# Low part of the first output-weight block of each group on VectorE instead of GpSimd, in a fused attention and feed-forward kernel

## The reference

```
q, k, v = xn @ wq, xn @ wk, xn @ wv      # 32 query heads, 8 key/value heads, 128 wide
q, k = rope(q), rope(k)
s = softmax(q k^T / sqrt(128), causal and at most 127 tokens back) v     # per head
s = s @ wo                                # 4096 x 512
g = silu(ffn(xn))                         # ffn: W1, W3, W2 from packed 4-bit values and scales, hidden 1376
out = x + s * g
```

## Time and profile before

| | |
|---|---|
| median of 3 runs | 816.35 us (816.35, 816.83, 815.01) |
| the profiled execution's own time | 816.31 us |
| its span, first to last instruction | 814.5 us |
| mean granted TensorE clock | 0.998 of full speed |
| TensorE busy | 799.0 us (98%), 3928 matmuls |
| VectorE busy | 564.8 us (69%) |
| GpSimd busy | 484.3 us (59%) |
| ScalarE busy | 428.2 us (53%) |
| GpSimd L398 on output weights, groups 1 to 7 | 28 of them |
| GpSimd L398 on input weights, all | 40 of 1393 ns |
| DMA | 54.00 MB, mean 66 GB/s |

### The profile page before, as it was taken

One profiled execution on the slowest core, in us unless ns is written; L12 is line 12 of the kernel. 1 busy time (PEld: TensorE's weight loads), 2 busy tenths in 40 slices (PEclk: granted clock), 3 DMA queues, 4 the chain that ended last, 5 costly groups with the idle time before them and its releaser, 6 DMA issues.

```text
span 814.5 us, 13389 instructions
## 1 busy us (share of the span) xinstructions
PE 799.0 (98%) x3928; PEld 668.5 (82%) x3928; DVE 564.8 (69%) x1628; ACT 428.2 (53%) x1103; POOL 484.3 (59%) x362
## 2 busy tenths in 40 slices
PE   6999999999999999999999999999999999999987
PEld 4888888888888888888888888888888888888876
DVE  6625858576558867767686777768677676867774
ACT  4412313223138675666656576665656666665562
POOL 2112324224156774877488497747839774789985
PEclk9999999999999999999999999999999999999999
DMA  9449525211000400400030040003004001220102
GB/s 286 147 164 271 157 78 139 82 39 52 0 28 14 130 14 0 131 1 14 12 118 13 0 129 0 13 28 101 13 0 129 0 13 38 91 64 0 39 1 104
DMA packets 51908, 54.00 MB, mean 66 GB/s; under 512 B 4128, under 2 KB 33184, under 8 KB 51872
## 3 DMA queue, kind: packets, MB, share of 16 engines
q1 hardware_dynamic: 51584, 53.49, 22.0%
q10 hardware_dynamic: 288, 0.07, 0.0%
HBM read 47.25 MB, written 6.29 MB: 66 GB/s over the span
## 4 chain that ended last, share of the span: by engine, by line
PE 75%; POOL 15%; issue 6%; DVE 1%; ACT 1%; DMA 0%; POOLq 0%; ACTq 0%; DVEq 0%
PE bank L1270 20%; PE bank L1271 20%; PE bank L1272 20%; POOL wol L398 5%; POOL swap L424 5%; PE bank L1384 2%; PE bank L1397 2%; PE bank L1311 2%; PE bank L1316 2%; PE bank L1322 2%; POOL q L428 2%; POOL pl L447 1%; POOL ph L447 1%; POOL acc L455 1%; PE bank L1414 1%
## 5 line engine op out<-in xcount | busy, mean ns | idle before, releaser
L424 POOL TENSOR_TENSOR swap<-swap,cst 128x512 f32<-128x512 f32 x80 | 108.4, 1355 | 39.6 <-ACT swap L665 39.6
L686 ACT ACTIVATE probs<-probs,nmx 128x128 f32<-128x128 f32 x256 | 100.0, 392 | 60.4 <-DVE nmx L1055 60.4
L1270 PE MATMUL bank<-xh,wih 128*128 128x512 f32 x320 | 128.9, 403 | 0.0
L1271 PE MATMUL bank<-xl,wih 128*128 128x512 f32 x320 | 125.2, 391 | 0.0
L1272 PE MATMUL bank<-xh,wil 128*128 128x512 f32 x320 | 125.0, 391 | 0.0
L1270 PE MATMUL bank<-woh,oh 128*128 128x512 f32 x256 | 100.5, 392 | 0.1
L1271 PE MATMUL bank<-wol,oh 128*128 128x512 f32 x256 | 100.2, 391 | 0.0
L1272 PE MATMUL bank<-woh,ol 128*128 128x512 f32 x256 | 99.9, 390 | 0.0
L374 POOL TENSOR_TENSOR hl<-act_h,hh 128x512 fp32r<-128x512 f32 x22 | 32.0, 1454 | 102.2 <-ACT hh L564 102.2
L428 POOL TENSOR_TENSOR q<-q,swap 128x512 f32<-128x512 f32 x64 | 85.5, 1335 | 6.7 <-DVE q L1030 1.8
L447 POOL TENSOR_TENSOR ph<-ph,cst 128x512 fp32r<-128x512 f32 x32 | 42.8, 1338 | 72.0 <-ACT ph L701 72.0
(11 more groups left out here) (121 smaller groups left out, 2006.5 us busy)
## 6 DMA issues: line engine op xcount, KB each, us to landing
raw<-in_wq SPq DMA_DIRECT2D x32, 256.0 KB, 5.0
raw<-in_wo SPq DMA_DIRECT2D x32, 256.0 KB, 4.9
pk<-in_w SPq DMA_DIRECT2D x44, 128.0 KB, 3.7
sc<-in_s SPq DMA_DIRECT2D x44, 128.0 KB, 3.9
vals<-stage SPq DMA_DIRECT2D x16, 256.0 KB, 2.5
vraw<-vals SPq DMA_DIRECT2D x16, 256.0 KB, 3.0
pk<-in_w SPq DMA_DIRECT2D x11, 256.0 KB, 2.7
sc<-in_s SPq DMA_DIRECT2D x11, 256.0 KB, 3.0
```

Source lines behind the costliest of these rows:

```text
L424: nc.gpsimd.tensor_tensor(v, v, spread(sin.unsqueeze(1), P, 2, SEQ), ALU.mult).then_inc(sin_done, 1)
L686: e = nc.scalar.activation(probs[:, s, c0:c1], probs[:, s, c0:c1], ACT.Exp, bias=nmx[:, s, i:i + 1], scale=-1.0, accum_out=rsum[:, s, i:i ...
L1270: nc.tensor.matmul(out_, sh, mh, start=(i == 0), stop=False)
L1271: nc.tensor.matmul(out_, sh, ml, start=False, stop=False)
```

## The change

In groups 1 to 7 the low part of the first output-weight block (`wol[:, 0]`) is made by VectorE, behind its two `p_lo` and ahead of `cos_part`, in step `bp` = 0. GpSimd's loop over the four blocks begins at the second. In group 0 GpSimd still makes all four. The low part of slot 5 counts a semaphore of its own, `wl_here`, on either engine, so that `wl_done` counts eight per group, and all waits on it are renumbered. SP and TensorE wait for `wl_here` where they need that block.

```diff
@@ constants
-ALL_W = CHUNKS * NKV
+LOWS = CHUNKS - 1
@@ semaphores
-        wh_done, wl_done = sem("wh_done"), sem("wl_done")
+        wh_done, wl_done, wl_here = sem("wh_done"), sem("wl_done"), sem("wl_here")
@@ counts
+        def wo_low(g, h):
+            return LOWS * g + (5 + h - 1)
+        def in_low(g, c):
+            return LOWS * g + c
@@ SP, group_loads
-                        wait(sp, wl_done, wo_chunk(g, h) - RING + 1)
+                        if h == 0:
+                            sp.wait_ge(wl_here, g)
+                        else:
+                            wait(sp, wl_done, wo_low(g - 1, h) + 1)
                         load_wo(5 + h, g, h)
...
-                        wait(sp, wl_done, in_chunk(g + 1, c) - RING + 1)
+                        wait(sp, wl_done, in_low(g, c) + 1)
                         load_in(c, g + 1, c)
@@ SP, reload of x at the end
-                sp.wait_ge(wl_done, ALL_W + t - RING + 1)
+                if t == 5:
+                    sp.wait_ge(wl_here, NKV)
+                else:
+                    sp.wait_ge(wl_done, (in_low(NKV - 1, t) if t < 5 else wo_low(NKV - 1, t - 5)) + 1)
@@ GpSimd, w_lo
-                nc.gpsimd.tensor_tensor(lo, raw[:, slot, :], hi.bitcast(f32), ALU.subtract).then_inc(wl_done, 1)
+                nc.gpsimd.tensor_tensor(lo, raw[:, slot, :], hi.bitcast(f32), ALU.subtract) \
+                    .then_inc(wl_here if slot == 5 else wl_done, 1)
@@ GpSimd, step
                 if w:
-                    for h in range(GH):
+                    for h in range(1, GH):
                         lo_wo(g, h)
@@ VectorE
+            def first_wo_lo(g):
+                dve.wait_ge(wh_done, wo_chunk(g, 0) + 1)
+                nc.vector.tensor_tensor(wol[:, 0, :], raw[:, 5, :], woh[:, 0, :].bitcast(f32),
+                                        ALU.subtract).then_inc(wl_here, 1)
@@ VectorE, step
                 p_lo(g, bp, 0, 0)
                 p_lo(g, bp, 0, 1)
+                if bp == 0:
+                    first_wo_lo(g)
                 cos_part(ng, nbp, 0)
@@ TensorE, project
-                    pe.wait_ge(wl_done, in_chunk(g, c) + 1)
+                    pe.wait_ge(wl_done, in_low(g, c) + 1)
@@ TensorE, out_project
                 if bp == 0 and t == 0:
-                    pe.wait_ge(wl_done, wo_chunk(g, GH - 1) + 1)
+                    pe.wait_ge(wl_here, g + 1)
+                    pe.wait_ge(wl_done, wo_low(g, GH - 1) + 1)
```

## The result

The changed kernel took 812.16 us (median of 6 runs, 811.16 to 813.01), the kernel before 816.82 in the runs beside it: ratio 0.9945, 95% interval 0.9930 to 0.9959. That is 4.7 us by the medians. The profiled execution took 811.49 us with a span of 809.7.

A forecast was written before the change was run, and what follows sets the result against it. TensorE, busy in 98% of the span, was taken as the bound, waiting for GpSimd's late masked copy. Six turns 2.7 + last group 1.0 + clock 1.4 = 5.1 us; 816.3 - 5.1 = 811.2 us, range 809.9 to 814.0.

The forecast's parts named there:

- The six turns: Groups 1 to 6: TensorE's 0.50 us wait per turn for GpSimd's masked copy shrinks by 0.45; 2.7 us (1.8 to 3.0).
- the last group: Group 7: GpSimd loses one of four low parts, so L1423 comes 0.9 to 1.4 us earlier; taken as 1.0 us.
- The clock term: TensorE's clock fall behind the last group's waits may not come: 1.4 us or nothing; clock still falling had chance 0.27.
- The next candidate: Product at 422.85, needing VectorE's low part from 421.50 to 422.19; moved up by 0.50, its start and that part are level.
- Only 0.6 of the 1.4 us come through: First masked copy, now at 419.15, can't start before 418.55 because of ScalarE's high part; GpSimd waits for the rest.
- VectorE for nothing in groups 1 to 6: Moved subtraction fits VectorE's 2.65 us gap behind the first two turned blocks; 0.68 to 1.34 us long, costed at nothing.
- The point from which it is paid: Slower outcome decides if the moved subtraction takes over 2.5 us or ScalarE's high part comes over 1.7 us after 398.8.
- The slower rival: VectorE becomes late, delaying key rotation, masking and low parts; 3.9 us over seven groups, 820.2 us; chance 0.05.
- Contention, up to 0.46, swallowed by the idle time: Moved instruction slows GpSimd's masked copy at 399.66 by up to 0.46 us; 0.82 us idle behind it absorbs that.
- the likeliest case: The forecast itself, 811.2 us, with the six turns, the last group and the whole clock term; chance 0.50.

The follow-up runs named there:

- half a block in place of a whole one: Kernel before, nothing moved; from group 1 on GpSimd makes only 256 of 512 columns of the first output-weight block's low part; 811.95 us (one run).
- the run with one column: Changed kernel with VectorE making only one of the 512 columns of the moved low part; 811.13 us, ratio 0.9944.
- last group undone: Changed kernel, but in group 7 GpSimd makes all four low parts, as before; 813.59 us, ratio 0.9969.
- the last two kernels: Changed kernel with two rest products behind the last group's last rotation, 809.84 us; then all four there and some sums moved later too, 809.20 us.

## Why the prediction was right

The forecast was 811.2, the profiled execution took 811.49 and the median is 812.16, in the stated range. The six turns and the last group came out as worked out. The clock term did not, and that the total is so close is in part luck.

- *Six turns, 2.7 us (1.8 to 3.0).* Measured 2.8 to 2.9, near the upper end: 0.49 per turn and not 0.45. The next candidate, VectorE's low part at 421.50, now ends at 420.83 + 0.69 = 421.52, and the product that needs it starts at 421.67 with no wait shown. It was level, as said, and TensorE did not have to wait for it.
- *Only 0.6 of the 1.4 us come through.* Right in kind: GpSimd waits 0.67 us in front of the masked copy, and half a block in place of a whole one gives 70.29. What comes off GpSimd behind the low parts is 1.7 us and not 1.3 to 1.5. The wait for ScalarE's swap, 0.58 us, was not in the working; it changed nothing, since the copy of the high part comes later still.
- *VectorE for nothing in groups 1 to 6.* Shown by the run with one column (0.53 us less, no gain) and by the run that does it twice (1.66 us more, no cost). The duration was 1.17 in the loop, 1.60 in the last group, of the 0.7 to 1.8 allowed. The point from which it is paid was put at 2.5 us of length; two instructions of 2.9 us together are still free in the loop, three of 4.6 cost 1.85 per turn.
- *The slower rival.* It did not come about, but its mechanism is real: 0.46 us over the kernel before when the instruction stands one place later, where the price worked out was 0.55 per group.
- *Contention, up to 0.46, swallowed by the idle time.* 0.44 in the loop, swallowed. In the last group it was paid: the copy takes 1.75 us and not 1.28, and the one-column run, which spares that, has L1445 0.37 us earlier.
- *The last group, 1.0 us.* 0.93.
- *The clock, 1.4 us or nothing.* This term was mis-sized. TensorE's clock did not fall in the profiled execution (granted 1.00 from 775 to 778 us), and L1445 to the second product of scores behind it took 778.38 - 774.70 = 3.68 us where it had been 783.59 - 778.63 = 4.96: 1.28 less. Of this, some 0.4 were given back between there and the next turning (784.98 - 778.38 = 6.60 us against 789.82 - 783.59 = 6.23), where TensorE, no longer slowed, stands for short times between the products of scores; one of these waits, 0.2 us, is shown, and it is for VectorE's masking. Three of the changed kernel's six runs had 1.000 or 0.999 and took 811.16 to 811.49, and three had 0.998 and took 812.83 to 813.01. The forecast gave the term whole to the likeliest case. But half of the changed kernel's runs still had the fall, and seven of 23 runs of the kernel before had none. On the mean the fall cost 0.9 us before (816.03 over all 23, 815.13 without it) and 0.8 in the changed kernel (812.10 over all six, 811.31 without it), so the term is worth about 0.1 us and not 1.4. The median of 812.16 lies between the two kinds. Without any fall on either side the gain is 815.04 - 811.27 = 3.8 us, the six turns and the last group. The 4.7 of the medians come against six runs of the kernel before with a median of 816.82; against its 23 others, with a median of 816.0, it is 3.8 too.

What stays open is why the clock falls in one execution and not in the next with the same waits. No run here was made to tell it. By kernel, with the three waits of its last group in the profiled execution, and a mean granted clock of 0.998 or less taken as a fall: it fell in 16 of 23 runs before (1.15, 0.73 and 0.49 us), in 7 of 8 with the last group undone (1.15, 0.74, 0.50), in 2 of 4 with the part made twice (1.09, 0.74, 0.39), in 3 of 6 of the changed kernel (0.64, 0.74, 0.50), in 1 of 4 with one column (0.23, 0.76, 0.50), and in none of the ten of the last two kernels, where no wait before these products reached 0.3 us. It falls less often as the waits get shorter, but with so few runs that is a hint and no more.

## What to carry to other kernels

A saving on an engine that is late is worth the wait of the bounding engine behind it and no more; read that wait by the starts of the instructions around it, then look who is next. An idle gap on another engine takes work for free only in its own place: one instruction later the same work turned a gain of 0.49 us per turn into a loss of 0.46. Where two engines take turns, as VectorE and GpSimd do here, every shift of one moves the other, so a saving is to be judged with the neighbours' durations and not alone. And a term that comes and goes from one execution to the next is to be counted by how often it is there, before and after, and not whole.

## What was not expected of the hardware

A VectorE subtraction of one column with both inputs in SBUF took 0.64 us in the loop and 1.06 in the last group, both times until the GpSimd instruction of 1.3 us that was under way had ended. A 512-column one took from 0.68 us (no GpSimd instruction under way) to 1.86, and in the changed kernel each of the 49 beside GpSimd ended 0.54 to 0.59 us after GpSimd's. With one input in PSUM none was longer than 0.69. GpSimd in its turn was held up by up to 0.5 us. A cut of some 0.3 us in GpSimd's work made one product on VectorE 1 us longer, and what stands behind it that much later.
